# A six-stage decoder kernel: where VectorE takes the second attention's statistics, how stage five scales its softmax, and how the last chunk is finished

## What is computed

```python
x = x + _L0_attn_ref(_layernorm(x), ...)                       # stage a
x = x + _L0_xattn_ref(_layernorm(x), ctx_1024, ctx_1024, 0, mask)   # stage b, 32 heads
x = x + _L0_ffn_ref(_layernorm(x), ...)                        # stage c
x = x + _L1_attn_ref(_layernorm(x), ...)                       # stage d
x = x + _L1_xattn_ref(_layernorm(x), ctx_1024, Wq, Wk, Wv, Wskip)   # stage e
x = x + _L1_ffn_ref(_layernorm(x), ...)                        # stage f

# stage e: softmax of energy / sqrt(64) over 64 channels, times v, plus skip
# stage f: h = relu(x @ up) ** 2; shared = h @ down; routed = latent path times the
#          sum of the two largest router logits; result layernorm(shared + routed) * gamma + beta
```

## Time and profile before

| | |
|---|---|
| median of 3 runs | 1232.08 us (1231.9 to 1233.46) |
| profiled execution | 1230.97 us, of which the span of the core is 1229.2 us |
| busy share of PE, DVE, ACT, POOL | 91%, 58%, 38%, 34% |
| chain that ended last, by engine | PE 61%, DVE 15%, ACT 5% |
| mean granted TensorE clock | 0.95 of 2.4 GHz |
| stage b | about 205 to 384 us |
| stage e | about 877 to 990 us |
| end of the last matmul, end of the span | 1207.3 us, 1229.2 us |

### The profile page before, as it was taken

The page is one execution under the profiler, slowest core; times in us unless marked ns, Lnnn a source line. Parts: engine busy times, 40 slices in busy tenths (PEclk is TensorE's granted clock), DMA queues, the critical chain, the costliest instruction groups (busy, mean ns, idle before and its releaser), DMA issues.

```text
span 1229.2 us, 23652 instructions
## 1 busy us (share of the span) xinstructions
PE 1115.0 (91%) x9380; PEld 594.6 (48%) x9380; DVE 708.2 (58%) x1255; ACT 463.2 (38%) x813; POOL 418.8 (34%) x365
## 2 busy tenths in 40 slices
PE   6788996999997879999999999999989799999992
PEld 3454453766675444444444444444555444444441
DVE  6777684788887674435214411522399824646456
ACT  4566572555554542422111211211356422222220
POOL 2345375888871320000370160000043300606053
PEclk9887786899999999999999999999999899999997
DMA  6000000111120220320020010000000000000000
GB/s 235 2 3 2 27 5 15 41 42 41 42 67 4 63 63 24 100 80 1 20 78 1 0 51 0 1 1 1 4 10 7 1 1 1 26 9 34 0 35 35
DMA packets 29011, 35.91 MB, mean 29 GB/s; under 512 B 5882, under 2 KB 20499, under 8 KB 28788
## 3 DMA queue, kind: packets, MB, share of 16 engines
q1 hardware_dynamic: 27506, 34.53, 8.9%
q10 hardware_dynamic: 1410, 0.06, 0.1%
HBM read 30.24 MB, written 4.19 MB: 28 GB/s over the span
## 4 chain that ended last, share of the span: by engine, by line
PE 61%; DVE 15%; ACT 5%; issue 2%; POOL 0%; DVEq 0%; ACTq 0%; POOLq 0%
PE p_up L116 10%; PE p_up L117 10%; PE p_up L118 10%; PE p_y L116 8%; PE p_y L118 8%; PE p_y L117 8%; DVE wf_lo L246 2%; ACT wd_hi L2277 2%; DVE e_den L2225 1%; DVE b_top L1360 1%; DVE e_top L2215 1%; PE p_up L110 1%; PE p_y L1517 1%; DVE X L1383 1%; PE p_up L1505 1%
## 5 line engine op out<-in xcount | busy, mean ns | idle before, releaser
L1916 DVE TENSOR_TENSOR d_h_low<-d_hf,d_h_high 128x512 f16<-128x512 f32 (+1 forms) x40 | 27.8, 696 | 205.1 <-ACT d_h_high L2005 205.1
L116 PE MATMUL p_up<-d_xt_high,wd_hi 128*128 128x512 f16 (+1 forms) x352 | 134.3, 382 | 2.9 <-PE p_y L118 1.5
L117 PE MATMUL p_up<-d_xt_low,wd_hi 128*128 128x512 f16 (+1 forms) x352 | 134.1, 381 | 0.0
L118 PE MATMUL p_up<-d_xt_high,wd_lo 128*128 128x512 f16 (+1 forms) x352 | 134.1, 381 | 0.0
L170 ACT ACTIVATE d_sg<-p_up 128x512 f32<-128x512 f32 (+1 forms) x40 | 23.7, 594 | 212.8 <-PE p_up L118 212.8
L116 PE MATMUL p_y<-wd_hi,d_h_high 128*128 128x512 f16 (+1 forms) x272 | 103.2, 380 | 0.0
L117 PE MATMUL p_y<-wd_lo,d_h_high 128*128 128x512 f16 (+1 forms) x272 | 103.2, 379 | 0.0
L118 PE MATMUL p_y<-wd_hi,d_h_low 128*128 128x512 f16 (+1 forms) x272 | 103.2, 379 | 0.0
L138 POOL TENSOR_SCALAR wd_raw<-wd_raw 128x1156 f32<-128x1156 f32 x8 | 25.1, 3137 | 208.6 <-DVE d_h_low L1916 208.6
L435 POOL TENSOR_TENSOR a_pt_low<-a_ex,a_pt_high 128x1024 f16<-128x1024 f32 x32 | 68.2, 2131 | 81.3 <-ACT a_pt_high L924 81.2
L2187 POOL TENSOR_TENSOR wd_hi<-wd_hi,e_den 128x1024 f32<-128x1024 f32 x16 | 30.5, 1908 | 152.3 <-DVE e_den L2227 152.3
(11 more groups left out here) (332 smaller groups left out, 2974.3 us busy)
## 6 DMA issues: line engine op xcount, KB each, us to landing
wd_raw<-in_w_d SPq DMA_DIRECT2D x16, 616.0 KB, 3.7
wd_raw<-in_w_f SPq DMA_DIRECT2D x8, 578.0 KB, 3.8
X<-in_x SPq DMA_DIRECT2D x4, 1024.0 KB, 12.2
wd_lo<-in_ctx_t SPq DMA_DIRECT2D x128, 32.0 KB
out_x<-wd_raw SPq DMA_DIRECT2D x16, 256.0 KB, 2.0
wd_lo<-in_ctx SPq DMA_DIRECT2D x32, 64.0 KB, 2.3
wd_raw<-in_w_c SPq DMA_DIRECT2D x1, 1096.0 KB, 12.5
wd_hi<-in_Wo SPq DMA_DIRECT2D x1, 1024.0 KB
```

What stands on the lines that cost most here:

```text
L116: nc.tensor.matmul(ps, st[0], mv[0], start=start, stop=False)
L117: nc.tensor.matmul(ps, st[0], mv[1], start=False, stop=False)
L118: return nc.tensor.matmul(ps, st[1], mv[0], start=False, stop=stop)
L1916: nc.vector.tensor_tensor(hid[1][0:n, d % NH, :], value, hid[0][0:n, d % NH, :], ALU.subtract).then_inc(h_ready, 1)
```

## The change

Four edits.

1. Stage b: `update` is cut in two. `add` (the residual) stays where it was, on odd n. `measure` (the two statistics instructions) moves behind the maxima and behind `low_x` of the following even n. `norm` and `low_x` are written elsewhere in the loop, but come at the same point of DVE's list.
2. Stage e: the factor 1/8 goes into ACT's copy of the keys, `tensor_reduce` gives the negated maxima, and `bias`, its instruction and its semaphore are gone. Exp now reads `top` directly, so `soft(t)` also waits for the exponentials of t - 2.
3. Stage f, last chunk, PE: blocks 6 and 7 are made for tiles 0 and 1 together, then for tile 2, then for tile 3.
4. Stage f, last chunk, the rest: POOL adds beta to the four tiles of X ahead of time. DVE takes the statistics in two pairs and computes (y - mean) * gamma; for tiles 0 and 1 ACT multiplies by the root and POOL adds X + beta; for tiles 2 and 3 one DVE instruction does both. POOL makes the roots of each pair. SP stores in the order 0, 2, 3, 1.

```diff
-                def update(t):
+                def add(t):
                     v.wait_ge(z_ready, 2 * t + 2)
                     nc.vector.tensor_tensor(held.X[:, t, :], held.X[:, t, :],
                                             o[:, t % 2, :, :, :, :].rearrange("p k q h d -> p (k q h d)"),
                                             ALU.add).then_inc(x_ready, 1)
+
+                def measure(t):
                     v.wait_ge(x_ready, t + 1)
...
                         norm_o(n - 2)
                         if n % 2:
-                            update(n // 2 - 1)
+                            add(n // 2 - 1)
                     if n + 2 < N:
                         peak(n + 2)
+                    if n >= -1 and n % 2 and n // 2 + 3 < NT:
+                        norm(n // 2 + 3)
+                    if n >= 0 and n % 2 == 0 and n // 2 + 2 < NT:
+                        low_x(n // 2 + 2)
+                    if n >= 4 and n % 2 == 0:
+                        measure(n // 2 - 2)
+                measure(NT - 1)
...
         v.wait_ge(s_ready, t + 1)
+        if t >= 2:
+            v.wait_ge(exp_ready, t - 1)
         nc.vector.tensor_reduce(top[:, b, :], score_banks(t).rearrange("p (j m) -> p j m", j=NJ), AX.X,
-                                ALU.max).then_inc(top_ready, 1)
-        v.wait_ge(top_ready, t + 1)
-        nc.vector.tensor_scalar(bias[:, b, :], top[:, b, :], -S ** -0.5, None, ALU.mult).then_inc(bias_ready, 1)
+                                ALU.max, negate=True).then_inc(top_ready, 1)
...
-            nc.scalar.activation(keys[half, t % 3, s, :], bank[half, 0:M], ACT.Copy)
+            nc.scalar.activation(keys[half, t % 3, s, :], bank[half, 0:M], ACT.Copy, scale=S ** -0.5)
...
+                store(NC - 1, 0, final, NT - TC + 1)
                 for i in range(LP, TC):
                     store(NC - 1, i, final_v, i - LP + 1)
-                for i in range(LP):
-                    store(NC - 1, i, final, TC * (NC - 1) + i + 1)
+                store(NC - 1, 1, final, NT - TC + 2)
...
+                pool.wait_ge(xn_ready, NT)
+                for t in range(NT - TC, NT):
+                    nc.gpsimd.tensor_tensor(held.X[:, t, :], held.X[:, t, :], held.bet[:], ALU.add).then_inc(based, 1)
...
+                root(0)
+                pool.wait_ge(based, TC)
+                for i in range(LP):
+                    t = NT - TC + i
+                    pool.wait_ge(normed, t + 1)
+                    nc.gpsimd.tensor_tensor(y[:, i, :], y[:, i, :], held.X[:, t, :], ALU.add).then_inc(final, 1)
+                root(1)
...
+                def weigh(i):
+                    v.wait_ge(y_steps, 2 * (NT - TC) + 4 * (i // 2) + 3 + i % 2)
+                    nc.vector.scalar_tensor_tensor(y[:, i, :], y[:, i, :], ymv[:, i, 0:1], held.gam[:], ALU.subtract,
+                                                   ALU.mult).then_inc(weighed, 1)
+
+                add_routed(NC - 1, (0, 1))
+                spread(0)
+                for i in range(LP):
+                    add_routed(NC - 1, (LP + i,))
+                    weigh(i)
+                spread(1)
+                weigh(2)
+                weigh(3)
+                v.wait_ge(yrs_ready, 2 * NC + 2)
+                v.wait_ge(based, TC)
+                for i in range(LP, TC):
+                    v.wait_ge(weighed, i + 1)
+                    nc.vector.scalar_tensor_tensor(y[:, i, :], y[:, i, :], yrs[:, i:i + 1], held.X[:, NT - TC + i, :],
+                                                   ALU.mult, ALU.add).then_inc(final_v, 1)
...
+                act.wait_ge(yrs_ready, 2 * NC)
+                for i in range(LP):
+                    act.wait_ge(weighed, i + 1)
+                    nc.scalar.activation(y[:, i, :], y[:, i, :], ACT.Copy, scale=yrs[:, i:i + 1]).then_inc(normed, 1)
...
+                def close_last(c):
+                    for tiles in ((0, 1), (2,), (3,)):
+                        down(c, FU - 2, tiles)
+                        down(c, FU - 1, tiles)
```

More of the change, by code:

```diff
@@ L1397, in vector @@
                         p.c.low(v, 1)
-                    if n >= 0 and n // 2 + 2 < NT:
-                        if n % 2:
-                            low_x(n // 2 + 2)
-                        else:
-                            norm(n // 2 + 2)
                     if 0 <= n < N:
@@ L2128, in part_e @@
     top = sb("top", [128, 2, NJ])
-    bias = sb("bias", [128, 2, NJ])
     den = sb("den", [128, 2, NJ])
@@ L2277, in expo @@
             last = nc.scalar.activation(prob[:, t % 3, j, :], scores[:, j, :], ACT.Exp,
-                                        bias=bias[:, t % 2, j:j + 1], scale=S ** -0.5)
+                                        bias=top[:, t % 2, j:j + 1])
         last.then_inc(exp_ready, 1)
@@ L2434, in finish @@
                     nc.gpsimd.tensor_tensor(yrs[:], yve[:], held.mhalf[:, 0:TC], ALU.pow).then_inc(yrs_ready, 1)
-                    for i in range(tiles):
+                    for i in range(TC):
                         t = TC * c + i
@@ L2499, in blocks, with add_routed @@
                                                 ALU.subtract).then_inc(h_ready, 1)
-                def add_routed(c):
-                    for i in range(TC):
+                def add_routed(c, tiles=range(TC)):
+                    for i in tiles:
                         t = TC * c + i
@@ L2539, in vector, with spread @@
                 blocks(NC - 1, False)
[L2540 to L2549 removed]
+                def spread(pair):
+                    at = 2 * (NT - TC) + 4 * pair
+                    for i in (2 * pair, 2 * pair + 1):
+                        v.wait_ge(y_read, NT - TC + i + 2)
+                        nc.vector.bn_stats(yst[:, i, :], y[:, i, :]).then_inc(y_steps, 1)
+                    for j, i in enumerate((2 * pair, 2 * pair + 1)):
+                        v.wait_ge(y_steps, at + j + 1)
+                        nc.vector.bn_aggr(ymv[:, i, :], yst[:, i, :]).then_inc(y_steps, 1)
+                def weigh(i):
[16 more added lines that the diff above has]
+                                                   ALU.mult, ALU.add).then_inc(final_v, 1)
             def scalar(act):
@@ L2637, in up, with down @@
                     last.then_inc(up_ready, 1)
-                def down(c, f):
+                def down(c, f, tiles=range(TC)):
                     pe.wait_ge(h_ready, FU * c + f + 1)
@@ L2655, in blocks, with close @@
                         down(c, f - 2)
+                def close(c):
                     down(c, FU - 2)
-                    if more:
-                        turn(c + 1)
+                    turn(c + 1)
                     down(c, FU - 1)
```

40 lines of the change are left out of this document (19 added, 21 removed).

## The result

| | before | changed |
|---|---|---|
| median | 1232.77 us (4 runs, 1231.9 to 1235.13) | 1217.05 us (4 runs, 1214.69 to 1220.05) |
| profiled execution, span | 1230.97, 1229.2 us | 1217.62, 1215.9 us |
| ratio | | 0.9871, 95% interval 0.9844 to 0.9897 |

The changed kernel is 1.3% faster. To see where, both traces are cut at the same six events: the first and the last residual of stage b (L1383, its tiles 0 and 15), the last residual of stage d, the last of stage e, the start of the last low part of a hidden block in stage f, and the end of the span. Here are these rows of DVE's timeline, before and then changed (start, length, engine, line).

What follows compares the result with a forecast made beforehand. Bounds: in stage b PE's wait for DVE's maxima, at the end DVE's chain behind the last matmul. 4.0 + 3.2 + 9.5 = 16.7 us off 1230.97 gives 1214.3, as median 1215.4 us; range 1209 to 1221, own range 1213 to 1218.

Steps and rivals of the forecast that it cites:

- Stage b, 4.0 us forecast: Stage b: statistics moved behind the maxima let PE gain until POOL holds it; 4.0 us, bounds 0 and 12.4.
- It gets a little faster: Stage b: POOL's L1315 meets DVE's residual less often in five early tiles; 5 x 0.34 = 1.7 us.
- the gain of 1.5 us up to the last scores: Stage b: PE can gain only POOL's lead at the last tile's keys, 1.54 us, taken as 1.5.
- 0.8 us more for the last maxima: End of stage b: the last maxima (n = 31), which no key holds back, come 0.8 us earlier.
- slower than before: Stage b rival, 2%: PE waiting for POOL falls to 1.2 GHz, 8 us a tile over eight tiles, time 1275.
- The rival by the rule: Stage b rival, 15%: residual and POOL's L1291 exclude each other, 0.5 us a tile eats the 4.0; time 1219.4.
- Stage e, 3.2 us forecast: Stage e: without the bias a tile takes 5.5 us, not 5.70; 1.7 + 0.9 + 0.65 = 3.2 us, bounds 0 and 7.3.
- a norm "near 0.9 us": Stage e, sign in the changed profile: DVE's norm L103 near 0.9 us long, as it waits for POOL.
- The rival by which a norm without delay would bring 7.3 us: Stage e rival, 12%: the norm isn't delayed and PE becomes the bound; 7.3 in place of 3.2, time 1211.3.
- The tail, 9.5 us forecast: Behind the last matmuls: the end comes at 1219.7 instead of 1229.2 us; 9.5 us, bounds 7.5 and 11.
- the waits at the first pair: Tail: weigh 0 may wait for POOL's roots, so weigh 1 ends at 1210.7 us, not 1209.9.
- The price of the order of tiles, 1.1 us: Tail, PE: the new tile order completes tile 0's sum some 1.1 us earlier.

Runs made afterwards that it cites:

- relief_after: The changed kernel with POOL's scaling of the values in stage b (L1304) given to ACT; 1203.84 us, ratio 0.977.
- e_alone: The kernel before with only stage e's bias folded into its keys; 1226.38 us, ratio 0.9961.
- e_and_tail: The changed kernel with stage b's statistics back ahead of the maxima as before; 1215.41 us, ratio 0.9869.
- tail_alone: The kernel before with only the changes to stage f's last chunk; 1218.44 us, ratio 0.9892.
- norm_late: The changed kernel with DVE's norm in stage e put behind the residual and its statistics; 1214.34 us, ratio 0.9854.
- tile_order: The changed kernel with PE's last two down projections in the old order, all four tiles of one, then of the other; 1211.35 us, ratio 0.9855.
- fill_after: The changed kernel with eight unused PE matmuls added ahead of each of stage b's last three attentions; 1215.91 us, ratio 0.9875.

## Why the prediction was right and wrong

The forecast, 1215.4 us, stands 1.65 us from the median, and both of its ranges hold it. That it came so near is in part luck. Of the 16.7 us of the sum the profiled execution shows 13.3. The largest error, stage b with 6.85 us (4.0 forecast, -2.85 measured), is partly covered by a tail that gave 1.3 more, a stage e that gave 0.55 more, and 1.6 us ahead of stage b that no edit made. The mechanism was right in stage e and in the tail. In stage b it was right that POOL comes next, and wrong what that leaves.

**Stage b, 4.0 us forecast, -2.85 measured.** The part of the step that named the next wait was right: PE's wait for the maxima at L1505 went (L1509 waits once, 1.3 us in all), the wait ahead of L1482 (now L1486) came in its place, with POOL's L1295 behind it (weight loads waited there 9.6 us in 12 tiles), and PE's own pace is 9.31 us a tile in relief_after against the forecast 9.34. POOL's last keys ended at 360.43 and not near 359.3, though this run was 1.6 us early. The first long wait came where it was said, at tile 8. The step failed at three places, which together are the loss of this execution.

First, *"It gets a little faster"*. POOL did not. From its first L1291 of the stage to the end of its last keys it took 155.75 us before and 156.70 in the changed kernel. The meetings at L1315 became fewer as foreseen (21.7 to 20.7 us in all), but others came in their place, about 2 us: L1304 was 0.85 us long in all of its 15 instances before and up to 1.09 now. Some of them meet DVE's norm, an instruction with one input that the working never asked about; others meet the residual, which was already running when L1304 began. Here are three of POOL's one-input instructions that grew (from 0.85, 0.85 and 1.56), each with the norm or the residual that it met:

```profile
264.01 0.54 DVE L103 TENSOR_SCALAR d_xn<-X,mv,rstd 128x512 f32<-128x512 f32 x1
264.17 1.08 POOL L1304 TENSOR_SCALAR wd_lo<-wd_lo 128x256 f32<-128x256 f32 x1 [0.20 <-POOL wd_lo L1295]
```

```profile
225.60 1.85 POOL L1291 TENSOR_SCALAR wd_lo<-wd_lo,mask_bs 128x512 f32<-128x512 f32 x1 [0.21 <-POOL wd_lo L1315]
226.46 0.54 DVE L103 TENSOR_SCALAR d_xn<-X,mv,rstd 128x512 f32<-128x512 f32 x1
```

The edit isn't the only thing that brings such meetings. With stage b as before, POOL's stretch took 155.72 us in e_alone and 155.87 in e_and_tail, but 156.62 in tail_alone, where the residual met L1304 in four tiles (up to 1.08 us long). With the edit it was 156.67 to 157.08 in five traces. So the edit costs POOL some 0 to 1 us, depending on how DVE and POOL stand to each other in the execution.

Second, the gain of 1.5 us up to the last scores needs a PE that is where POOL is. At 330 us it was, by the row above. At the last tile its scores began at 362.61, 2.2 us behind the end of the keys (359.27 + 1.16 = 360.43), more than the 1.54 of before. In between lies the fall of the clock from 330 to 340 us, in which a tile took PE longer than POOL, and it had not caught up by the end. In norm_late, with the same code in stage b and the same wait of 2.69 us at tile 12 (to 325.95), the clock stayed up for the next 10 us. It fell only behind a further wait of 1.10 us (to 336.52), and was back at 1.00 after some 4 us:

```profile
326.00:336.00 10.00, 9.41 (x224) 6.96 (x224) 7.68 (x13) 5.29 (x9) 8.50 (x9) 1.00 0.17 45
338.00:343.00 5.00, 5.00 (x95) 4.29 (x87) 2.92 (x5) 1.45 (x3) 4.30 (x6) 0.66 0.23 67
```

There PE was waiting for POOL again at the last tile (keys ready at 356.78, scores from 356.87), so the 1.5 us up to the last scores did come; POOL's longer stretch (157.08 us) took most of it back, and stage b was 146.92 us. tile_order went the same way. So this part of the loss hangs on how long the clock stays low behind a wait, and why that was 9 us in the one case and 4 in the other, the runs don't show.

Third, *"0.8 us more for the last maxima"*: from tile 13's residual to tile 15's it took 14.02 us before and 15.24 now, with the clock at 0.50 from 374 to 384. fill_after, with the clock up, took 14.16, so the low clock is some 1.1 of these 1.2 us.

These are 0.95, 0.64 and 1.22, in all 2.8 of the 2.85 us that the profiled execution lost. The prediction had the mechanism of the last two as its rival "slower than before", with 2%: PE waiting for POOL falls to 1.2 GHz. It was right that PE's clock falls and wrong in the price: not 8 us in each of eight tiles, but two stretches of 7 and 10 us at the low clock, most of which POOL's own pace hides. Its argument against (PE idles 0.69 us a tile at a clock of 1.00) looked at the wrong idle time. What came is rarer and longer: PE catches up with POOL at its own pace (9.31 us a tile in relief_after), and then stands for 2.69 us at once behind POOL's roots, which the working had named ("a root every fourth tile on top") and not counted as a wait of PE.

**The rival by the rule.** The rule on the shared port that the prediction weighed (the Trainium skill, SBUF — State Buffer, section "SBUF: two separate sides") gave a stage b without gain (15%), and that came out. Its reason is part of it. The prediction tested the rule in one order only, the residual beginning within POOL's one-input instruction, and its working from there was too general. Late within L1291 the residual is as long as alone; early within it, it is longer by 0.27 us, and still ends ahead of POOL's instruction:

```profile
280.10 1.57 POOL L1291 TENSOR_SCALAR wd_lo<-wd_lo,mask_bs 128x512 f32<-128x512 f32 x1
281.31 0.69 DVE L1383 TENSOR_TENSOR X<-X,wf_lo 128x512 f32<-128x512 f32 x1
```

```profile
271.30 1.57 POOL L1291 TENSOR_SCALAR wd_lo<-wd_lo,mask_bs 128x512 f32<-128x512 f32 x1 [0.21 <-POOL wd_lo L1295]
271.57 0.96 DVE L1383 TENSOR_TENSOR X<-X,wf_lo 128x512 f32<-128x512 f32 x1
```

In the other order, with the residual under way when POOL's one-input instruction begins, POOL pays. L1304 took 1.09 us at 253.27 (above), and in norm_late L1291 took 2.03 us where 1.56 is normal:

```profile
332.86 0.69 DVE L1383 TENSOR_TENSOR X<-X,wf_lo 128x512 f32<-128x512 f32 x1
332.95 2.03 POOL L1291 TENSOR_SCALAR wd_lo<-wd_lo,mask_bs 128x512 f32<-128x512 f32 x1 [0.21 <-POOL wd_lo L1295]
```

The trace before has a row of the first order too: the residual at 288.06 took 0.76 us, 0.18 us into L1304. So in these rows POOL waits when DVE is first, as by the rule, and DVE doesn't wait for the whole instruction when POOL is first. The Trainium skill, SBUF — State Buffer (section "SBUF: two separate sides"), also counts a DVE instruction in a two-port mode among those that exclude GpSimd. No run here shows whether the norm is such an instruction; what its meetings cost stands in the last section.

**Stage e, 3.2 us forecast, 3.75 and 3.3 measured** (changed kernel and e_alone). Right, and by its steps: the norm took the bias's place in waiting for POOL, and the residual starts 0.20 us behind POOL's end (924.48), as taken. The tile is 5.40 us and not 5.5, since without the bias the way from the residual to the sums is 1.76 and not 1.87. The sign of it that was named, a norm "near 0.9 us", was off: it is 1.23, as it starts when the bias did. The rival by which a norm without delay would bring 7.3 us is gone too: norm_late made it, and stage e gained nothing, since PE is next.

**The tail, 9.5 us forecast, 10.8 measured.** Right in all places, short in size. From the last low part, forecast and measured: first addition 1.66 and 1.61, first roots done 6.2 and 5.5, tile 1 weighed 8.0 and 6.9, second statistics 9.7 and 8.3, second roots done 12.3 and 11.0, DVE's end 13.6 and 12.5. The mis-sized term is that of the waits at the first pair: two roots take POOL 0.71 us and not 1.0, and weigh is 0.74 us long in both tiles, so the 0.8 us of waits that were taken there did not come. Where POOL adds X and DVE weighs, at 1208.45, they did (2.23 us for two). The price of the order of tiles, 1.1 us, was measured at 1.0 to 1.1. The "some 9 us" from the last matmul to DVE's last instruction were 7.7.

## What to carry to other kernels

A wait removed on one engine is worth at most what the next engine is ahead by, and that can be read beforehand: here POOL's last keys were ready 1.54 us before PE took them, and the 9.6 us came only with an instruction moved from POOL to ACT. When an engine that has been paced evenly is let loose against a fixed one, look for the one long wait that takes the place of many short ones, because PE's clock may fall behind it. Here that wait came where the fixed engine had work that isn't in every turn of the loop, the roots. And cut both traces at the same events before believing a sum: totals that agree can hide terms of both signs. A stage's own length should come from more than one trace: with the same code stage b took 146.92 and 149.84 us.

## What the runs showed of the hardware that was not expected

- Before, PE idled up to 1.0 us in 13 tiles of stage b (0.69 ahead of 301.11), and its clock stayed at 1.00 from 296 to 378. In the changed kernel an idle time of 2.69 us (to 286.56, and to 330.07) was followed by a clock of 0.54 on the mean from 288 to 295 and 0.51 from 330 to 340. The same idle time in norm_late (to 325.95) was followed by 10 us at 1.00:

```profile
288.00:295.00 7.00, 7.00 (x100) 4.93 (x92) 4.54 (x8) 2.75 (x5) 6.09 (x7) 0.54 0.20 57
330.00:340.00 10.00, 9.93 (x118) 6.69 (x118) 4.43 (x8) 2.64 (x4) 8.38 (x9) 0.51 0.15 43
```

- Filling those gaps kept the clock up only as long as they were filled: behind the last added matmul it stood at 1.00 until the next idle time, and fell to 0.67 on the mean from 385 to 390.
- A one-input DVE instruction (the norm, SBUF to SBUF) often lengthens one-input instructions of POOL, by 0.14 to 0.29 us in the changed kernel, and waits up to 0.7 us for a two-input one. It doesn't always: in tail_alone it began at 236.50, 0.49 us into an L1291, and both took their normal times (0.54 and 1.56 us).
- A two-input DVE instruction (the residual of stage b) that is already running lengthens a one-input instruction of POOL that begins beside it (1.09 for 0.85 us, 2.03 for 1.56). If POOL's began first, the residual was 0.27 us longer in one of the two rows shown and not longer in the other.
- DVE's residual of stage e, with its second input in PSUM, ran its normal 0.69 us at 918.29 in norm_late, the last 0.4 us of POOL's multiplication (from 916.81 for 1.90) beside it.
